# The head of a two-layer graph kernel: three x tiles and half of the key weights load ahead of the edges, edge selection behind the first key projection

## The reference, cut

```python
h = relu(layernorm(x))
# layer 0: graph convolution and attention (8 heads of 64, 256 random features) on h
xn  = batchnorm(h, n1g, n1b)
agg = segment_sum(xn[src], dst) / max(deg, 1)
conv = relu(agg @ W_conv + b_conv)
q, k, v = heads(h_dense @ Wq), heads(h_dense @ Wk), heads(h_dense @ Wv)   # h_dense: the first 256 rows
attn = feature_attention(q, k, v, proj) @ Wo
x = x + batchnorm(conv + attn + h, n2g, n2b)
# layer 1: sum of neighbours and a two-layer perceptron
h = relu(layernorm(x))
z = (1 + eps) * h + segment_sum(h[src], dst)
z = relu(batchnorm(z @ W1 + b1, g1, be1)) @ W2 + b2
x = x + h + relu(batchnorm(z, g2, be2))
```

## Time and profile before

| | us |
|---|---|
| median of 3 runs | 343.99 |
| lowest, highest | 342.71, 344.62 |
| profiled execution | 341.79 |
| its span, first to last instruction | 340.0 |
| PE, DVE, ACT, POOL busy | 327.1, 218.9, 165.7, 116.6 |

### The profile page before, as it was taken

How to read it: one execution, slowest core, us unless ns; L and a number is a source line. 1 busy time by engine, 2 the same in 40 slices (tenths; PEclk the granted TensorE clock), 3 DMA queues, 4 the chain that set the end, 5 groups by cost and what they waited for, 6 DMA issues and landing times.

```text
span 340.0 us, 5788 instructions
## 1 busy us (share of the span) xinstructions
PE 327.1 (96%) x2106; PEld 210.1 (62%) x2106; DVE 218.9 (64%) x486; ACT 165.7 (49%) x265; POOL 116.6 (34%) x200
## 2 busy tenths in 40 slices
PE   8999899999999999999798989999999999999994
PEld 4678556777676667765566654555555555566562
DVE  3979998987989559789787864213664444332325
ACT  2457867363471694633677754124444562513032
POOL 4323179553200010000427877231666643101100
PEclk9999999999999999999999999999999999999999
DMA  6994306000000000855000000000000000020223
GB/s 200 266 232 166 124 4 213 37 2 1 2 3 2 2 3 1 247 162 145 0 3 0 2 2 2 2 0 2 1 1 2 0 3 0 0 62 15 75 62 90
DMA packets 13480, 18.15 MB, mean 53 GB/s; under 512 B 1542, under 2 KB 6848, under 8 KB 13444
## 3 DMA queue, kind: packets, MB, share of 16 engines
q1 hardware_dynamic: 13095, 17.40, 18.4%
q10 hardware_dynamic: 349, 0.26, 0.2%
HBM read 15.10 MB, written 2.56 MB: 52 GB/s over the span
## 4 chain that ended last, share of the span: by engine, by line
PE 77%; DVE 12%; POOL 4%; issue 3%; ACT 3%; DVEq 0%; POOLq 0%; ACTq 0%
PE bank L1431 73%; PE bank L1467 2%; DVE st_f L1114 2%; POOL hn L556 1%; PE bank L1830 1%; DVE hT L1199 1%; DVE tmpr L1197 1%; POOL ln_s L516 1%; DVE rdb L1067 1%; PE bank L1789 1%; DVE st_row L1319 1%; ACT hh L846 1%; PE bank L1647 1%; DVE x L1382 1%; DVE st L1119 0%
## 5 line engine op out<-in xcount | busy, mean ns | idle before, releaser
L1431 PE MATMUL bank<-AT,hh 125*128 125x400 f16 (+3 forms) x250 | 81.2, 332 | 1.0 <-DVE hl L1300 0.6
L1431 PE MATMUL bank<-AT,hl 125*128 125x400 f16 (+3 forms) x250 | 80.8, 331 | 0.0
L1431 PEld LDWEIGHTS bank<-AT,hh 125*128 125x128 f16 x250 | 24.1, 97 | 19.3 <-issue 1.1
L1431 PEld LDWEIGHTS bank<-AT,hl 125*128 125x128 f16 x250 | 24.3, 97 | 17.8 <-issue 0.2
L1431 PE MATMUL bank<-a_hi,w_hi 128*128 128x400 f16 (+1 forms) x96 | 32.6, 339 | 0.0
L1431 PE MATMUL bank<-agg_hi,w_hi 128*128 128x400 f16 (+1 forms) x96 | 32.6, 339 | 0.0
L1431 PE MATMUL bank<-a_hi,w_lo 128*128 128x400 f16 (+1 forms) x96 | 32.5, 338 | 0.0
L1431 PE MATMUL bank<-agg_hi,w_lo 128*128 128x400 f16 (+1 forms) x96 | 32.5, 338 | 0.0
L1431 PE MATMUL bank<-agg_lo,w_hi 128*128 128x400 f16 (+1 forms) x96 | 32.5, 338 | 0.0
L1431 PE MATMUL bank<-a_lo,w_hi 128*128 128x400 f16 (+1 forms) x96 | 32.5, 338 | 0.0
L606 POOL TENSOR_TENSOR a_lo<-zr,a_hi 128x1250 f16<-128x1250 f32 x7 | 22.0, 3140 | 16.7 <-DVE a_hi L1353 16.7
(11 more groups left out here) (224 smaller groups left out, 716.6 us busy)
## 6 DMA issues: line engine op xcount, KB each, us to landing
w_s<-w SPq DMA_DIRECT2D x4, 1024.0 KB, 5.3
x<-x SPq DMA_DIRECT2D x2, 1120.0 KB
x_in<-x SPq DMA_DIRECT2D x4, 448.0 KB
out<-x SPq DMA_DIRECT2D x6, 224.0 KB
wB<-wk SPq DMA_DIRECT2D x1, 1024.0 KB, 8.8
wA<-wq SPq DMA_DIRECT2D x1, 1024.0 KB, 12.5
wC<-w_conv SPq DMA_DIRECT2D x1, 1024.0 KB, 12.9
wB<-wv SPq DMA_DIRECT2D x1, 1024.0 KB, 8.9
```

What stands on the lines that cost most here:

```text
L1431: return pe.matmul(o, l, r, start=start, stop=stop, skip_group_check=True)
```

## The change

SP begins with the x tiles 0, 1 and 2, each on its own, and the first half of wk's columns, none of which waits for `s_pad`. Then it waits for `s_pad` and issues all eight edge DMAs, the sources too, and then the second half of wk and tile 3. wk gets a semaphore for each half, and wv one of its own. ACT issues no DMA at the head; it loads its table by a copy of a constant, and makes edge16 behind the transposed copies of the first three tiles. DVE takes the statistics of tiles 0 to 2 first, then `first`, `falls`, tile 3's statistics and the flag, and only then reads the chosen edges. TensorE's products for `firsts` and `chosen` stand behind K0; the 7 fillers behind `chosen` are gone, and hT1 has 4 in place of 2.

```diff
-SPARE = {"start": 18, "chosen": 7, "hT0": 3, "hT1": 2, "hT2": 3}
+SPARE = {"start": 18, "hT0": 3, "hT1": 4, "hT2": 3}
...
-    take("chosen1", 2)
-    take("chosen0", 4)
-    take("firsts", 3)
...
+            if name == "K0":
+                take("firsts", 7)
+                take("chosen1", 5)
+                take("chosen0", 4)
...
         def _(sp):
+            def key_weights(half):
+                cols = slice(half * D // 2, (half + 1) * D // 2)
+                sp.dma_start(wB[:, :, cols], w_t(wk)[:, :, cols]).then_inc(sem(f"d_wk{half}"), 16)
+
+            for i in range(3):
+                load_tile(sp, i)
+            key_weights(0)
             sp.wait_ge(sem("s_pad"), 1)
-            for rows in EDGE_LOADS:
-                load_edges(sp, 0, *rows)
-            load_x(sp, 0)
-            load_tile(sp, 2)
-            sp.dma_start(wB[:], w_t(wk)).then_inc(sem("d_wB"), 16)
+            for a in range(2):
+                for rows in EDGE_LOADS:
+                    load_edges(sp, a, *rows)
+            key_weights(1)
             load_tile(sp, 3)
...
         def _(act):
-            act.wait_ge(sem("s_pad"), 1)
-            for rows in EDGE_LOADS:
-                load_edges(act, 1, *rows)
-            for a, name in enumerate(("d_dst", "d_src")):
-                act.wait_ge(sem(name), 16 * len(EDGE_LOADS))
-                act.activation(edge16[:, a, :], edge[:, a, :], ACT.Copy).then_inc(sem("s_edge16"), 1)
+            act.wait_ge(sem("s_ones"), 1)
+            act.activation(tables[:], ones16[:, 0:1], ACT.Copy)
...
             rows_T(1)
             rows_T(2)
+            for a, name in enumerate(("d_dst", "d_src")):
+                act.wait_ge(sem(name), 16 * len(EDGE_LOADS))
+                act.activation(edge16[:, a, :], edge[:, a, :], ACT.Copy).then_inc(sem("s_edge16"), 1)
             rows(3)
             attention("K0")
...
         def _(dve):
             dve.memset(edge[96:L, :, EROW:], PAD_DST).then_inc(sem("s_pad"), 1)
+            for i in range(3):
+                row_stats(i)
             dve.wait_ge(sem("d_dst"), 16 * len(EDGE_LOADS))
...
-            for i in range(3):
-                row_stats(i)
             own.step(dve.tensor_tensor(fall[:], edge[:, 0, 0:EROW], edge[:, 0, 1:EROW + 1], ALU.is_gt))
             dve.tensor_reduce(falls[:], fall[:], AX.X, ALU.max).then_inc(sem("s_falls"), 1)
+            row_stats(3)
...
+            irregular_flag()
...
             one_hots(0)
             local_destinations()
-            row_stats(3)
-            irregular_flag()
             dve.wait_ge(sem("s_flag"), 1)
...
                 for name in SLOTS[t]:
                     attention(name)
-                    if name == "hT1":
+                    if name == "K0":
+                        pe.wait_ge(sem("s_first"), 1)
                         first_granules()
+                        chosen_edges()
                     keep_busy(SPARE.get(name, 0), banks[0])
```

More of the change, by code:

```diff
@@ L422, in x_landed @@
         def x_landed(eng, i):
-            eng.wait_ge(sem(f"d_x_{i}" if i in (2, 3) else f"d_x{i // 2}"), 32)
+            eng.wait_ge(sem(f"d_x_{i}" if i < 4 else f"d_x{i // 2}"), 32)
         def store(eng, f, j, r):
@@ L453, in _ @@
             sp.wait_ge(full[PLACE["K1"][0]], PLACE["K1"][1] + 1)
-            sp.dma_start(wB[:], w_t(wv)).then_inc(sem("d_wB"), 16)
+            sp.dma_start(wB[:], w_t(wv)).then_inc(sem("d_wv"), 16)
             sp.wait_ge(full[PLACE["Q1"][0]], PLACE["Q1"][1] + 1)
@@ L939, in _ @@
             dve.memset(edge[96:L, :, EROW:], PAD_DST).then_inc(sem("s_pad"), 1)
[L940 to L948, removed]
             def row_terms(i):
@@ L961, in _, with irregular_flag @@
                 row_stats(i)
+            dve.wait_ge(sem("d_dst"), 16 * len(EDGE_LOADS))
+            own.step(dve.tensor_copy(keys[:], edge[:, 0, 0:EROW + GRAN:GRAN]))
+            own.step(dve.memset(keys[0:1, 0:1], -1.0))
+            dve.wait_ge(sem("s_from"), 1)
+            own.step(dve.tensor_tensor(below[:], lane_from[0:L].unsqueeze(1).broadcast_to([L, GPR + 1, LANES]),
+                                       keys[:].unsqueeze(2).broadcast_to([L, GPR + 1, LANES]), ALU.is_gt))
+            dve.tensor_tensor(first[:, :, 0:LANES], below[:, 0:GPR, :], below[:, 1:, :], ALU.subtract)\
+               .then_inc(sem("s_first"), 1)
             own.step(dve.tensor_tensor(fall[:], edge[:, 0, 0:EROW], edge[:, 0, 1:EROW + 1], ALU.is_gt))
             dve.tensor_reduce(falls[:], fall[:], AX.X, ALU.max).then_inc(sem("s_falls"), 1)
+            row_stats(3)
+            def irregular_flag():
+                ps = read_group(dve, "firsts")
+                own.mark(dve.memset(from_row[:, LANES:], float(EROW * L // GRAN - 1)))
+                own.mark(dve.tensor_copy(from_row[:, 0:LANES], ps[0:1, 0:LANES]))
+                own.step(dve.tensor_copy(n_falls[:], ps[0:1, P:P + 1]))
+                dve.sem_inc(free[PLACE["firsts"][0]], 1)
+                own.step(dve.tensor_tensor(span_row[:], from_row[:, 1:], from_row[:, 0:LANES], ALU.subtract))
+                own.step(dve.tensor_reduce(longest[:, 0:1], span_row[:], AX.X, ALU.max))
+                own.step(dve.tensor_scalar(longest[:, 1:2], longest[:, 0:1], float(REACH - 1), None, ALU.is_gt))
+                own.step(dve.tensor_tensor(irregular[:], longest[:, 1:2], n_falls[:], ALU.add))
+                dve.sem_inc(sem("s_flag"), 1)
+            irregular_flag()
             def twice(a):
@@ L988, in edges_of_destinations @@
                                           ALU.is_equal).then_inc(sem("s_edges_of"), 1)
[L990 to L1001, removed]
             def pairs(a):
@@ L1439, in _ @@
             keep_busy(SPARE["start"], banks[0])
[L1440 to L1453, removed]
             pe.wait_ge(sem("s_const"), NCONST)
@@ L1461, in first_granules, with chosen_edges @@
                 close_group(mm(ps[0:1, P:P + 1], falls[:], ones16[0:L, 0:1], True, True), "firsts")
+            def chosen_edges():
+                lanes_of = [open_group(pe, f"chosen{a}")[:, 0:CHUNKS * LANES] for a in range(2)]
+                pe.wait_ge(sem("s_base"), 3)
+                mm(lanes_of[0], ones16[0:1, :], lane_base[:], True, False)
+                mm(lanes_of[1], tile_len[:], src_base[:], True, False)
+                pe.wait_ge(sem("s_edge16"), 2)
+                for a in (1, 0):
+                    for c in range(CHUNKS):
+                        o = lanes_of[a].rearrange("p (h c) -> p c h", c=CHUNKS)[:, c, :]
+                        for g in range(GPR):
+                            e0 = g * GRAN + c * P
+                            ins = mm(o, edge16[:, a, e0:e0 + P], first[:, g, 0:LANES], False, c == CHUNKS - 1 and g == GPR - 1)
+                    close_group(ins, f"chosen{a}")
             def turn_rows(i, rows, slots, h_done, name):
@@ L1559, in attention @@
                     nt = int(name[1])
-                    pe.wait_ge(sem("d_wB"), 32)
+                    pe.wait_ge(sem("d_wv"), 16)
                     ps = open_group(pe, name)
@@ L1564, in attention @@
                 elif name in ("Q0", "Q1", "K0", "K1"):
-                    w, d, n = (wA, "d_wA", 16) if name[0] == "Q" else (wB, "d_wB", 16)
-                    pe.wait_ge(sem(d), n)
+                    w, d = (wA, "d_wA") if name[0] == "Q" else (wB, f"d_wk{name[1]}")
+                    pe.wait_ge(sem(d), 16)
                     ps = open_group(pe, name)
```

## The result

| | kernel before | changed kernel |
|---|---|---|
| median of the runs made side by side, us | 343.19 (20) | 345.19 (20) |
| ratio | | 1.0063, interval 1.0046 to 1.0080 |
| profiled execution, us | 341.79 | 345.46 |
| its span, us, and granted TensorE clock | 340.0, 0.999 | 343.7, 0.993 |

The changed kernel is slower, by 2.0 us in the medians and by 3.67 us between the two profiled executions. The two differ because single executions of either kernel scatter by more than a microsecond, and the profiled one of the kernel before is the lowest of its twenty, where the other lies near its kernel's median. Of the 20 of the changed kernel, four with a mean granted clock of 0.998 took 343.3 to 344.1 us, the other sixteen, at 0.984 to 0.995, took 344.5 to 348.1. The ratio is the one on record for these runs; the quotient of the two medians is 1.0058.

What follows compares the result with a forecast made beforehand. The prediction took TensorE's in-order chain, hinging on the end of window 0's counts, as the bound. Counts +2.15 and hT4 +0.3 made +2.45, rounded 2.5, on a median of 343.99: 346.5 us, range 344.6 to 348.8.

Steps and rivals of the forecast that it cites:

- K0 earlier: TensorE's K0, hanging on x tile 2, starts at 10.5 in place of 14.04, a gain of 3.5 us.
- What stands behind K0: On TensorE, firsts and chosen products, formerly hidden, now follow K0 and cost 2.95 us, done at 17.05.
- K0's road to the counts: K0, small products, then 2.3 us of DVE's code2, S and ring: window 0's counts at 19.35, +1.4.
- Tile 3's road decides: DVE's statistics of tile 3 and the flag precede chosen; landing at 14.2, counts start at 20.1, +2.15; 55 in 100.
- the forecast's own 5.9 us: From tile 3's landing to window 0's counts: 2.5 for statistics and flag, 3.3 for chosen to ring, 0.1 for semaphores.
- the bytes behind wk: On the DMA queue, 0.25 MB behind wk at wk's own pace puts tile 3's landing 1.3 us later.
- the allowance for rows of 1 KB: wk's DMA rows are 1 KB, not 2 KB, unpriced; a reason to take tile 3's landing at 14.2.
- The rival with K0's road: Tile 3 lands by 13.4, so only K0's +1.4 and 0.1 for hT4 remain: 345.5; 20 in 100.
- Behind the counts: DVE's dst2, flag load and window 1's one-hots delay tile 4's hring, so TensorE's hT4 waits 0.3 us more.
- The clock: Rival: TensorE's clock falls in a 3 us hole and K1 runs at half clock, +3.7, 350.2; 4 in 100.
- POOL's hn: Rival, not slower: DVE's split no longer runs beside POOL's four hn, 3.2 us come back, 343.3; 10 in 100.
- The sum: +2.45, rounded 2.5: profiled execution 341.79 + 2.5 = 344.3, median 343.99 + 2.5 = 346.5.

Runs made afterwards that it cites:

- fillers: Changed kernel plus twelve TensorE products on constants, results unread, behind the chosen edges: 343.53 us, ratio 1.0033 to the kernel before.
- tile 3 late: Changed kernel with tile 3's statistics moved back behind dst2 on VectorE: 344.94 us, ratio 1.0065 to the kernel before.
- K1 in the hole: Changed kernel with K1 issued ahead of window 0's counts: 344.86 us, ratio 1.0059 to the kernel before.
- one tile ahead: Kernel before with x tile 0 loaded ahead of the edges, its statistics first on VectorE, wk in halves: 342.07 us, ratio 0.9979.
- without the fillers: Kernel with one tile ahead, minus the seven filler products behind the chosen lanes: 342.02 us, ratio 0.9956 to the kernel before.
- flag first: Kernel with one tile ahead, run without the fillers, and the irregular flag ahead of tile 3's statistics on VectorE: 340.95 us, ratio 0.9942.
- three tiles ahead: Changed kernel with firsts and chosen lanes between hT2 and K0, edges ahead of wk, sources by ScalarE, tile 3 behind dst2: 342.29 us, ratio 0.9980.

## Why the prediction was right in its time and wrong in its road

The number (346.5, range 344.6 to 348.8, slower by over 0.5%) holds: 345.19, slower by 0.63%, though the interval (0.46 to 0.80%) reaches under 0.5%. By its steps:

- **K0 earlier.** Forecast 10.5, measured 10.91. Tiles 0 and 1 landed at 3.54 and 4.94, tile 2 at 6.36 in place of 5.4, and K0 hangs on tile 2. The half of wk was no wait, as said.
- **What stands behind K0.** Forecast 2.95 us for firsts and chosen lanes; measured from K0's end, at 14.5, to about 17.5. The order and the size are right.
- **K0's road to the counts.** Forecast K0 + 8.85, measured K0 + 9.08, the same in three kernels (changed, fillers, tile 3 late). The chosen lanes ended at 17.53, K0 + 6.62 (forecast 6.55), and from there to the counts it was the hole of 2.46 (forecast 2.3, which is what code2, S and ring take, with nothing for the hand-over at either end). The flag, at 15.03 to 16.45, was no part of it: behind it VectorE waited 0.16 for TensorE. With K0's 0.41 the misses make +2.04 instead of +1.4.
- **Tile 3's road decides.** This is the step that failed. I took its landing at 14.2, the upper end of 12.8 to 14.3; it landed at 13.10, near the lower end (13.60 in the execution with the fillers). By the forecast's own 5.9 us its road would have given 19.0, a microsecond ahead of the 19.99 that came. Of the arguments for the upper end the bytes behind wk were right: wk's second half landed at 6.63 + 5.4 = 12.0, and tile 3 came 1.1 behind it (forecast 1.3). What was wrong is wk's own landing, 0.8 ahead of the lower bound of 12.8, and the allowance for rows of 1 KB, of which nothing shows. (The 2.44 MB that the forecast puts ahead of tile 3 are those up to its end; 2.2 stand ahead of it.) I had taken the moment when VectorE looked (14.81, without a wait) for a sign of the landing, which it wasn't. The rival with K0's road, given 20 in 100, is what happened, mis-sized as above. The experiment that moves tile 3 shows it.
- **Behind the counts.** Forecast 0.3 for hT4; measured nothing. With K1 at full clock (the fillers) the eight transposes still start without a wait and take 1.03 us as in the earlier trace rows. A reason is that the flag's load, 0.74 in the earlier trace rows, cost nothing: window 1's S followed at 20.44 at once.
- **The clock.** I gave its fall 4 in 100, since no row that I had read showed it, and priced it at 3.7. (The trace of before does have the lower level, in its last microsecond: 0.58 from 339 to 340, with TensorE at rest since 335.93.) It fell in the head in this profile and in those with tile 3 late and with K1 in the hole, behind holes of 2.46, 2.46 and 1.69 us, and in none of the other seven. Holes of 1.37 (one tile ahead, ahead of the chosen lanes) and of 1.47 (ahead of hT8, in all ten) were not followed by it. It cost K1 1.68 and not 3.7, since the half clock made one group of 16 products 5.37 us long. The Trainium skill, "TensorE: Matmul & The Clock Gate", "What's actually happening", says that TensorE drops to half its clock after idling: the trace agrees in kind, and I weighed the page far too low against one row that showed an idle stretch without a fall.
- **POOL's hn** didn't move: 4.91 us beside VectorE's split, as the argument against that rival said.
- **The sum.** The profiled execution was forecast at 344.3 and took 345.46: 1.16 too low. The clock makes +1.57 of it from counts to counts, the counts -0.11, hT4 -0.30 and the rounding of 2.45 to 2.5 another -0.05, which leaves 0.05. The median was forecast 1.3 too high. It was built on 343.99, a median of three; twenty executions gave 343.19. And the profile of before was one in which the clock did not fall until its last microsecond, which isn't so for all executions behind its median; so two profiles differ by more than the medians. That the time came out well inside the range is luck: the road was the wrong one and still ended within 0.1 us of the counts' start, and a base 0.8 too high and a clock left out pull in opposite directions. The rival whose road it was gave 345.5, nearer to 345.19, and left the clock out too.

## What to carry to other kernels

Loads turned round are worth what the last of the engines that need them can take: here K0 came 3.1 us earlier and the counts, for which everything waits, 2.0 us later, because work that had run in a stretch where TensorE had nothing to do was put on the path. Move the data forward and leave the cover where it is; then look for the fillers and the small waits that the old timing had hidden: without the fillers the kernel ran 0.4% under the one before, and 0.6% with the flag first. And where a change opens a hole on TensorE ahead of a dense stretch, price the half clock behind it with a chance that counts, whatever one quiet row says.

## What the runs showed of the hardware

The clock falls behind a hole or in it, and not after every hole of a kind. TensorE's timeline of the kernel before around 168 us:

```profile
169.51 0.48 PE L1431 MATMUL bank<-ident,hT 128*125 128x128 f32 x2 [1.81 <-DVE hT L1282]
...
173.77 0.35 PE L1431 MATMUL bank<-AT,hh 125*128 125x450 f16 x1
```

The same of the kernel with one tile ahead and no fillers:

```profile
169.07 0.48 PE L1440 MATMUL bank<-ident,hT 128*125 128x128 f32 x2 [1.80 <-DVE hT L1291]
...
175.00 0.35 PE L1440 MATMUL bank<-AT,hh 125*128 125x450 f16 x1
```

and its busy time by stretch there:

```profile
168.00:169.00 1.00, 0.00 (x0) 1.00 0.00 0
169.00:170.00 1.00, 0.93 (x5) 0.87 0.00 0
170.00:171.00 1.00, 1.00 (x6) 0.50 0.00 0
...
172.00:173.00 1.00, 1.00 (x4) 0.50 0.06 16
173.00:174.00 1.00, 1.00 (x8) 0.93 0.00 0
```

From the hole's end to the products on AT it took 5.93 us where the kernel before took 4.26: 1.67, the same price as K1's in the head. Half of it comes back: from these products to POOL's first a_lo (L606; L613 here) it is 64.77 us before and 63.93 here, where TensorE's later waits are shorter (0.42 in place of 0.90 ahead of the transposes at 181). One place, one length of hole, two outcomes: of ten profiled executions, all with a hole of 1.79 to 1.81 us there, three show the fall (this one, the one with the flag first and the one with three tiles ahead). In this one it comes 0.7 us after TensorE took up work again, in the one with three tiles ahead at about 169.6, in the last tenths of the hole, which ends at 169.75. In the head it came 1.5 us after (21.5, the changed kernel). What decides isn't settled by these runs. It is a likely source of the two groups in which the kernel before's own executions lie, but that is argued, since some executions with a full clock were slow as well.

The transfers show no loss by the change of order or of row length. Each half of wk took 5.4 us from issue to landing, so that the last of wk was there at 12.0 (13.3 before), and tile 3, behind the same bytes as before, at 13.10. The destinations, now behind three tiles and half of wk, were there at 9.46 and not 4.83, and the eight edge issues on one queue ran from 3.71 to 6.59; neither delayed anything on the road to the counts, since TensorE reached the firsts only at K0's end. With one tile ahead, and the edges ahead of wk, the halves of wk took a median of 6.9 us.
